# Row maxima of causal attention: score products over four heads and 128 keys in place of one head and 512 keys

## What is computed

```python
q = rope(x @ Wq + bq)                    # 32 heads of 8
k, v = rope(x @ Wk + bk), x @ Wv + bv    # 8 groups of 8; four heads share a group
scores = q @ k.T / sqrt(8)               # 1024 x 1024 for each of 32 heads
scores = where(kpos > qpos, -inf, scores)
out = softmax(scores) @ v
x = x + out @ Wo + bo
```

## Time and profile before

| | |
|---|---|
| median of three runs | 797.16 us |
| profiled execution, its own time | 796.24 us |
| its span | 794.4 us |
| TensorE busy | 735.7 us (93%), 4776 matmuls |
| VectorE busy | 460.9 us (58%) |
| ScalarE busy | 373.9 us (47%) |
| L807, the reductions, x384 | 188.1 us busy |
| L994, their products, x384 | 105.8 us busy |
| L992, their masks, x256 | 55.2 us busy |
| attention | about 255 to 555 us of the span |

### The profile page before, as it was taken

One profiled execution on the slowest core, in us unless ns is written; L12 is line 12 of the kernel. 1 busy time (PEld: TensorE's weight loads), 2 busy tenths in 40 slices (PEclk: granted clock), 3 DMA queues, 4 the chain that ended last, 5 costly groups with the idle time before them and its releaser, 6 DMA issues.

```text
span 794.4 us, 13291 instructions
## 1 busy us (share of the span) xinstructions
PE 735.7 (93%) x4776; PEld 391.3 (49%) x4776; DVE 460.9 (58%) x942; ACT 373.9 (47%) x569; POOL 189.7 (24%) x158
## 2 busy tenths in 40 slices
PE   4699999999996677999999999997879999999997
PEld 2356666656564233333333434543446656556665
DVE  6555454545548977899988877643533333333334
ACT  6434343333334466746657667776622222222222
POOL 1273333333344412000000000000143333333332
PEclk9999999999998689999999999999699999999999
DMA  5353333334310000000000000000042222221212
GB/s 170 101 148 112 119 119 113 113 120 133 116 54 1 0 1 1 1 1 1 1 2 1 1 1 2 1 1 1 2 112 77 67 65 72 60 79 53 79 53 80
DMA packets 16169, 44.37 MB, mean 56 GB/s; under 512 B 2658, under 2 KB 5090, under 8 KB 16132
## 3 DMA queue, kind: packets, MB, share of 16 engines
q1 hardware_dynamic: 12388, 33.65, 14.4%
q10 hardware_dynamic: 3744, 10.23, 3.9%
HBM read 42.68 MB, written 1.19 MB: 55 GB/s over the span
## 4 chain that ended last, share of the span: by engine, by line
PE 82%; DVE 6%; issue 4%; ACT 4%; DMA 2%; POOL 1%; SPq 1%; DVEq 0%; ACTq 0%; POOLq 0%
PE psum L857 53%; PE psum L1021 8%; PE psum L1005 8%; PE psum L994 7%; PE psum L992 2%; PE psum L1008 2%; DVE m_part L807 2%; PE psum L979 1%; ACT kT L563 1%; PE psum L1028 1%; DMA coef_dram<-oT 1%; POOL R L379 1%; DVE kaug L797 1%; DMA R<-coef_dram 1%; DMA x_res<-x_dram 1%
## 5 line engine op out<-in xcount | busy, mean ns | idle before, releaser
L857 PE MATMUL psum<-xT,W_hi 128*128 128x512 f16 x880 | 265.2, 383 | 0.0
L379 POOL TENSOR_TENSOR R<-R 128x512 f32<-128x512 f32 x112 | 152.5, 1363 | 298.0 <-DVE R L718 250.1
L807 DVE TENSOR_REDUCE m_part<-psum 128x1 f32<-128x512 f32 (+3 forms) x384 | 188.1, 550 | 42.3 <-PE psum L994 40.1
L704 DVE SCALAR_TENSOR_TENSOR R<-psum,R 128x512 f32<-128x512 f32 x108 | 74.7, 691 | 226.0 <-ACT R L491 225.9
L491 ACT ACTIVATE R<-psum 128x512 f32<-128x512 f32 x108 | 64.4, 597 | 265.5 <-PE psum L857 265.5
L857 PE MATMUL psum<-W_hi,R 128*128 (+1 forms) x896 | 166.5, 275 | 11.5 <-DVE R L718 11.5
L578 ACT ACTIVATE R<-psum 128x1024 f32<-128x1024 f32 x144 | 141.8, 1024 | 68.1 <-PE psum L1005 45.6
L857 PE MATMUL psum<-xT,W_lo 128*128 128x512 f16 x440 | 168.2, 382 | 0.0
L857 PEld LDWEIGHTS psum<-xT,W_hi 128*128 (+1 forms) x880 | 86.8, 99 | 83.4 <-issue 3.5
L857 PE MATMUL psum<-W_lo,R 128*128 (+1 forms) x448 | 123.3, 275 | 0.0
L994 PE MATMUL psum<-kT,qT 128*128 128x512 f16 (+3 forms) x384 | 105.8, 334 | 1.0 <-DVE m_part L807 0.6
(11 more groups left out here) (101 smaller groups left out, 457.3 us busy)
## 6 DMA issues: line engine op xcount, KB each, us to landing
R<-coef_dram SPq DMA_DIRECT2D x64, 256.0 KB, 3.8
w_stage<-w_dram ACTq DMA_DIRECT2D x26, 384.0 KB, 2.9
R<-coef_dram SPq DMA_DIRECT2D x8, 448.0 KB, 3.5
R<-coef_dram SPq DMA_DIRECT2D x8, 384.0 KB, 3.4
R<-coef_dram SPq DMA_DIRECT2D x8, 320.0 KB, 3.5
R<-coef_dram SPq DMA_DIRECT2D x8, 192.0 KB, 3.7
x_res<-x_dram SPq DMA_DIRECT2D x8, 128.0 KB, 2.2
R<-coef_dram SPq DMA_DIRECT2D x8, 128.0 KB, 3.1
```

Of the source, the lines that this page charges most:

```text
L379: nc.gpsimd.tensor_tensor(hc[:, c, :], v[:, j, c, :], C[:, j, c * CH:(c + 1) * CH], ALU.mult).then_inc(s_hc[c], 1)
L704: nc.vector.scalar_tensor_tensor(out=v[:, j, c, :], in0=bank[2 + c][:, :], scalar=1.0 / WS, in1=sg[:, c, :], op0=ALU.mult, op1=ALU.mult).t ...
L807: nc.vector.tensor_reduce(m_part[:, h, kc:kc + 1], ps[:, 0:n], axis=AX.X, op=ALU.max).then_inc(free_of(e), 1)
L857: ins = nc.tensor.matmul(o, stat(a, k), mov(b, k), start=first and n == 0, stop=last and n == 3 * k_parts - 1, **kw)
```

## The change

The m events cover a quad (four heads) and one block of 128 keys: one product of 512 columns whose moving operand takes 128 columns from each of four key groups. VectorE reduces the bank to four maxima a row. There is one mask product of 512 columns for each quad, at the diagonal block. `m_part` holds up to 8 values a head, joined by one reduction for t >= 1. The planner's stream and its costs change with it: UH heads became GQ = 4 quads.

```diff
@@ attention_schedule: stream 0 @@
-        for h in range(NH):
-            for kc in range(t // 4 + 1):
-                streams[0].append(("m", k, i, h, kc))
+        for quad in range(GHI * GQ):
+            for kt in range(t + 1):
+                streams[0].append(("m", k, i, quad, kt))
                 k += 1
-            if h % UH == AHEAD - 1 and late:
+            if quad % GQ == AHEAD - 1 and late:
                 streams[0].append(("q2", late.pop()))
-            if h % UH == UH - 1:
-                u = 2 * i + h // UH
+            if quad % GQ == GQ - 1:
+                u = 2 * i + quad // GQ
                 streams[0].append(("mx", u))
@@ work @@
         if kind == "m":
-            cols = min(4, ORDER[e[2]] + 1 - 4 * e[4]) * P
-            return [(PE, 0.06 + cols / 2400), (DVE, 0.07 + cols / 960)], [("q1", e[2])]
+            return [(PE, 0.45 if e[4] == ORDER[e[2]] else 0.23), (DVE, 0.6)], [("q1", e[2])]
@@ build @@
-        m_part = sb("m_part", [P, NH, 2], F32)
+        m_part = sb("m_part", [P, NH, TT], F32)
-        last_m = {2 * e[2] + e[3] // UH: e for e in events if e[0] == "m"}
+        last_m = {2 * e[2] + e[3] // GQ: e for e in events if e[0] == "m"}
@@ VectorE @@
-                    n = min(4, t + 1 - 4 * kc) * P
-                    u = 2 * i + h // UH
-                    if (h % UH, kc) == (0, 0) and u >= 2:
+                    u = 2 * i + quad // GQ
+                    if (quad % GQ, kt) == (0, 0) and u >= 2:
                         dve.wait_ge(s_m, u - 1)
-                    nc.vector.tensor_reduce(m_part[:, h, kc:kc + 1], ps[:, 0:n], axis=AX.X,
+                    nc.vector.tensor_reduce(m_part[:, quad * GLO:(quad + 1) * GLO, kt],
+                                            ps.rearrange("p (g n) -> p g n", g=GLO), axis=AX.X,
                                             op=ALU.max).then_inc(free_of(e), 1)
                     m_all = m_part[:, h, 0]
-                    if t >= 4:
+                    if t >= 1:
                         if u >= 1:
                             dve.wait_ge(s_m, u)
-                        link(nc.vector.tensor_tensor(m_row[:], m_part[:, h, 0], m_part[:, h, 1], ALU.max))
+                        link(nc.vector.tensor_reduce(m_row[:], m_part[:, h, 0:t + 1], axis=AX.X, op=ALU.max))
                         m_all = m_row[:]
@@ TensorE @@
-                    g = h // (GQ * GLO) * GLO + h % GLO
-                    n = min(4, t + 1 - 4 * kc) * P
-                    diag = kc == t // 4
-                    if diag:
-                        nc.tensor.matmul(out_bank[:, n - P:n], identb[:], maskb[:, 0, :],
-                                         start=True, stop=False, skip_group_check=True)
-                    nc.tensor.matmul(out_bank[:, 0:n], qT1[:, i % 2, h // GLO, :],
-                                     kT[:, g, kc * 512:kc * 512 + n], start=not diag, stop=True,
-                                     skip_group_check=diag).then_inc(full, 1)
+                    to = out_bank.rearrange("p (g n) -> p g n", g=GLO)
+                    heads = slice(quad // GQ * GLO, (quad // GQ + 1) * GLO)
+                    if kt == t:
+                        nc.tensor.matmul(to, identb[:], maskb[:, 0, :].unsqueeze(1).to_broadcast([P, GLO, P]),
+                                         start=True, stop=False)
+                    nc.tensor.matmul(to, qT1[:, i % 2, quad, :], kT[:, heads, kt * P:(kt + 1) * P],
+                                     start=kt != t, stop=True).then_inc(full, 1)
```

More of the change, by code:

```diff
@@ L799, in _ @@
                 elif kind == "m":
-                    _, k, i, h, kc = e
-                    t = ORDER[i]
+                    _, k, i, quad, kt = e
                     ps = filled(dve, e)
-                    n = min(4, t + 1 - 4 * kc) * P
-                    u = 2 * i + h // UH
-                    if (h % UH, kc) == (0, 0) and u >= 2:
+                    u = 2 * i + quad // GQ
+                    if (quad % GQ, kt) == (0, 0) and u >= 2:
                         dve.wait_ge(s_m, u - 1)
-                    nc.vector.tensor_reduce(m_part[:, h, kc:kc + 1], ps[:, 0:n], axis=AX.X,
+                    nc.vector.tensor_reduce(m_part[:, quad * GLO:(quad + 1) * GLO, kt],
+                                            ps.rearrange("p (g n) -> p g n", g=GLO), axis=AX.X,
                                             op=ALU.max).then_inc(free_of(e), 1)
@@ L983, in _ @@
                 elif kind == "m":
-                    _, k, i, h, kc = e
+                    _, k, i, quad, kt = e
                     t = ORDER[i]
-                    if (h, kc) == (0, 0):
+                    if (quad, kt) == (0, 0):
                         taken(pe, ("q1", i))
-                    g = h // (GQ * GLO) * GLO + h % GLO
-                    n = min(4, t + 1 - 4 * kc) * P
-                    diag = kc == t // 4
-                    if diag:
-                        nc.tensor.matmul(out_bank[:, n - P:n], identb[:], maskb[:, 0, :],
-                                         start=True, stop=False, skip_group_check=True)
-                    nc.tensor.matmul(out_bank[:, 0:n], qT1[:, i % 2, h // GLO, :],
-                                     kT[:, g, kc * 512:kc * 512 + n], start=not diag, stop=True,
-                                     skip_group_check=diag).then_inc(full, 1)
+                    to = out_bank.rearrange("p (g n) -> p g n", g=GLO)
[5 more added lines that the diff above has]
+                                     start=kt != t, stop=True).then_inc(full, 1)
                 elif kind == "st":
```

## The result

| | median us | over before | 95% interval |
|---|---|---|---|
| before | 797.8 (4 runs) | | |
| changed | 802.3 (4 runs) | +0.48% | 0.30 to 0.67% |
| changed, again, five rounds | 802.1 (6 runs) | +0.61% | 0.46 to 0.76% |

The forecast was 799.0 us, 791.5 to 805.5. The change costs 4 to 5 us. The side and the range were right, the size was not: +1.8 us was forecast, less than half of the +4.5 measured. Its profiled execution took 802.31 us, with a span of 800.5.

A forecast was written before the change was run, and what follows sets the result against it. TensorE was taken to bound attention after 352 us, with VectorE pacing one hole before. Terms -0.5 - 0.3 - 0.6 + 1.0 + 2.15 = +1.8 us gave 799.0 us against the median of 797.16, range 791.5 to 805.5.

The forecast's parts named there:

- TensorE is the bound behind 352 us: Attention after 352 us: only fewer columns or holes on TensorE shorten the end; TensorE busy 57.8 of 58.0 us.
- The rival that VectorE was the bound: Attention: waits on VectorE were real and each saved reduction shows; 791.5 us, chance 0.14.
- Products, masks, reductions and mx: Score maxima in attention: products -0.5, masks -0.3, tile 2's reductions -0.6, joining maxima ahead of the hole's end +1.0 us.
- Four outputs: VectorE reduction to four maxima: taken at 0.60 us, like one output; rival at 0.80, some 824 us, chance 0.03.
- Four pieces: Score product's moving operand from four separate key groups: taken as 0 us extra.
- the upper bound: Operand in four pieces, each priced as its own product: 0.005 us, x 288 = 1.4 us slower.
- The late q2: Tile 7's first unit: q2 behind 8 products, not 2; six more reductions, 3.6 us, leave 2.15 us new idle.
- Unit 4 was taken alone: Only tile 7's first unit was charged, 2.15 us; rival that more q2 are late: up to 804.5 us, chance 0.17.
- work that TensorE does in the hole: Hole at tile 7's first unit: six products and a longer mask done early, 1.45 us taken off 3.6.
- the clock: Rival: the longer hole near 350 us brings a half-clock stretch, 3.4 us more, 802.4 us; chance 0.07.
- the other units: Units 2, 3 and 5: their late q2 taken as free, units 2 and 3 absorbed by the hole, 5 not yet needed.
- The weight load rival: Narrow masks of before: each costs its 0.099 us weight load, so the change is 11.5 us faster, 786; chance 0.02.

The follow-up runs named there:

- the early-q2 kernel: Changed kernel with q2 of every finished unit behind the next unit's first two products instead of its whole first quad; 797.4 us, -0.03% against before.
- unit 4's q2 early: Changed kernel with only the q2 of tile 7's first unit put behind two products, all other q2 left late; 798.5 us, +0.07% against before.
- the first eight experiments: Follow-up variants of the changed kernel or the kernel before, in q2 place, event order, reduction price, masks or reduced columns; 791.7 to 807.7 us.

## Why the prediction was right, and what it missed

*TensorE is the bound behind 352 us.* Held. With 65.5 us of VectorE's work away, TensorE was as full as before, and the stretch from tile 7's first block to the next layer norm was 2.2 us shorter than before; its own work away shortened the end. The rival that VectorE was the bound fell with the same run, whose own expectation for it was 20 us or more against the 10 measured. The list of waits had 52.9 us of weight loads held up by reductions; making these shorter by more than a third (684 to 425 ns) gave back a fifth of that.

*Work.* Products, masks, reductions and mx were put at -0.5 - 0.3 - 0.6 + 1.0 = -0.4 us; the early-q2 kernel measured -0.2, within its interval. Four outputs cost nothing: 0.60 from one reduction to the next, 684 ns each. Four pieces cost nothing that can be seen either. Where nothing holds them up, the next start comes 0.21 to 0.22 us behind such a product:

```profile
348.27 0.38 PE L991 MATMUL psum<-kT,qT 128*128 128x512 f16 x1
348.48 0.39 PE L1033 MATMUL psum<-ident,o_hl 128*128 128x128 f16 x4
```

The 0.005 us each of the upper bound are less than these rows resolve.

*The late q2.* Place and mechanism were right: q2 of tile 7's first unit stands 3.6 us behind its mx, as worked out. Unit 4 was taken alone, and it has 3.7 of 4.9 us. **The term that was mis-sized is this one:** +2.15 us was forecast and +4.9 measured, or +3.7 for unit 4 alone. Three parts were off.

First, 1.45 us were taken off for work that TensorE does in the hole and need not do later. Nothing of it came back: from tile 7's first block to the last score product the changed kernel took 193.8 us without a low stretch, against 193.7 with unit 4's q2 early. Part of the reason is in the lists. Only four more products and one more mask stand ahead of that block than with q2 early (97 and 21 against 93 and 20), not six: with q2 early, three products stand between it and the block, with q2 late only one. And tile 2's output projection, ahead of the block with q2 early, comes behind it in the changed kernel. First the list with unit 4's q2 early, then the changed kernel:

```profile
348.89 0.82 PE L855 MATMUL psum<-qkvo_h,oTT 128*128 128x256 f16 x6
```

```profile
370.81 0.82 PE L855 MATMUL psum<-qkvo_h,oTT 128*128 128x256 f16 x6
```

The delay of the block itself came out smaller than 3.6: 2.8 us (107.7 against 104.9). So without the clock, unit 4's q2 costs an estimated 2.9 us by these points, not 2.15.

Second, the clock was left out, as a rival with a chance of 0.07. Both profiled executions of the changed kernel have a low stretch between 300 and 360 us, which cost 1.0 us in one and 1.4 in the other, as read from the table (single executions); doubling the products brought 1.5 by the medians. The rival's price of 3.4 us was taken from 6.8 us at 1.2 GHz; the stretch at 353 us had half of that (0.66 over 5 us). Its evidence, that the shorter hole of before left the clock at 1.00, was no guide to where a low stretch falls. Whether the hole causes it stays open: the same hole was followed by none in the repeat. The kernel before has executions with a lower clock too: in the 32 runs beside the first eight experiments, the eight with a mean clock of 0.964 took 799.2 to 800.4 us, the others (0.966 to 0.969) 795.7 to 798.9.

Third, the other units, counted as absorbed, have 1.1 us by the medians, within the intervals. Together these are 5.0 us, an estimate from single executions and differences of medians, beside the 4.9 measured.

The Trainium skill, TensorE: Matmul & The Clock Gate, Part 1, says that the array is throttled unless activity releases it. The trace agrees in so far as the low stretch at 353 us follows 4.5 us in which TensorE was busy for 2.7; in the repeat 2.6 busy us of 4.5 were followed by a clock of 1.00, so no run here shows which activity decides.

*The weight load rival.* Fell: 256 narrow masks taken away brought 5.0 us and not 22 or more.

## What to carry to other kernels

When pieces of work are regrouped, look at every rule of the order that counts in pieces. "Behind the first one" moved a transposition from two products to eight behind its input, and undoing that took the whole cost away. Taking work from an engine that isn't the bound pays little, however long the list of waits on it is: 65.5 us less of VectorE's work paid 10, about half of it ahead of the stretch that TensorE bounds. Read the starts of the other engine first. And do not take work off the price of a hole because it runs inside it, before the new list shows that this work really moved ahead and nothing moved back in exchange.

## What was not expected of the hardware

A list with more matmuls was not slower, and by the medians faster: seven products issued twice, 802.1 to 800.6 us. Less work for TensorE in a stretch that is half idle was partly given back by the clock: without masks, the granted clock from 256 to 300 us was 0.69 in place of 0.81. And the low stretches move between executions of one program: one of the changed kernel has it at 353 us and a span of 800.5, the other near 315 us and a span of 799.0.
